# Reordering the attention turns of a two-layer macaron block: k, output projection, v's halves and a split evacuation

## The chip, the cores and the metric

One NeuronCore of a Trainium2 chip runs the whole program. The metric is device microseconds of one execution; the kernel before took 996.61 us (median of 3 runs, 995.93 to 996.84). The profile is of one further execution, of 997.68 us.

## The reference, cut to what matters

Activations are 4 sequences of 512 tokens of width 128. Layer 0 is half an FFN, attention, half an FFN; layer 1 is half a mixture of experts, attention, half a mixture of experts. Both attentions are causal with 16 heads of 64:

```python
q, k, v = x @ Wq, x @ Wk, x @ Wv                    # 128 -> 16 heads x 64
sim = where(causal, -max, q @ k.T * 64 ** -0.5)     # per head, 512 x 512
out = softmax(sim) @ v                              # row maxima are subtracted
out = sigmoid(x @ Wg) * out                         # in layer 0's attention alone
x = x + out @ Wout (+ b_out)                        # b_out in layer 1's attention
```

Every f32 matrix product is made of three f16 products: each operand is split into a high and a low half (high by high, high by low, low by high).

## The kernel before

An attention is 32 items: 4 sequences by 8 pairs of heads. An item passes six stages, one turn apart (`LAGS`): p projects q, k and v; m finds row maxima; s computes scores and exponentials; v multiplies by v's halves and evacuates; o splits the output in halves and turns it by a DMA; z is the output projection. `TURNS` is 37, and in turn t the item of stage p is t, of stage m is t-1, and so on. Turns 5 to 31 hold all six stages. All engines walk the same turns, each with its own instruction order written out by hand in a `body(t)`; semaphores tie them together. `FILL` puts a piece of other work (a transposition of normalized tokens, an FFN "up" or "down" projection, gate, routing) into some turns; `STATS` puts layer norm statistics at the end of some.

What the orders of one turn hold, with the lines of the profile:

- TensorE: scores(0) (L1926 to L1936), maxima(0) (L1890), project_q (L1735 to L1737, through `split_mm`), project_k, project_out (L1975 to L1977), scores(1), maxima(1), project_v, the fill, scores(2), maxima(2), outputs(0) (L1959 to L1961), max_rows (L1901), outputs(1). Where `late_k(a, t)` holds (stages p and s are present and the turn has no fill: 27 of 64 turns) project_k stands behind maxima(1) instead.
- ScalarE: exps(0) (L1009), q_high (L1030), k_high (L1035, behind exps(1) where late), output_high (L1042), exps(1), p_high (L1017), the fill's part, exps(2), minus_max (L1058), v_high (L1049), layer norm (L907), expert weight quarters (L954, L955, first attention, turns 2 to 25).
- VectorE: maxima(0) (L1345), q_low (L1352), k_low (L1358, behind maxima(2) where late), maxima(1), output_low (L1369), add_out (L1409, every eighth turn), maxima(2), the fill's part, evacuate (L1391 in the first attention alone, L1395, L1399), v_low (L1375), statistics (L1211, L1214).
- GpSimd: per item three subtractions for the low halves of the exponentials (L821) and two casts for high halves (L819); the quarters' low halves (L720) and the norm's rstd.
- SP: one transposing DMA per item (L626); it waits for output_low and for the project_out of the item before.

PSUM: q and v share bank 0, so project_q waits for v_low of the item before and project_v for q_low. k is in bank 7, which outputs(1) and the fill use too. So project_k waits for the last evacuation, and outputs(1) for k_low, or in turns with a fill for the fill's reader on VectorE. outputs(0) writes bank 6, outputs(1) bank 7; one evacuation, behind outputs(1), reads both. The output projection accumulates over eight items in bank 1. The scores use banks 4 and 5, so scores(u) waits for the exps before it. scores(0) waits for minus_max of its item, made in the turn before.

Of the kernel before, what the change touches and what calls it, by code (L numbers as in the profile page):

```python
# [24 lines left out]
ALU = mybir.AluOpType  # L25
# [6 lines left out]
def macaron_block(nc: bass.Bass, ins, out, phases):  # L32
    tokens = ins["L0_attn_tokens"]
    NB, SEQ, D = tokens.shape
    P = 128
    TOK = NB * SEQ
    NT = TOK // P
    TPB = SEQ // P
# [29 lines left out]
    with ctx:  # L68
# [3 lines left out]
        def sem(name):  # L72
            return ctx.enter_context(nc.semaphore(name))
# [263 lines left out]
        s_pl_last = sem("pl_last")  # L337
        s_pl = sem("pl")
        s_av_ps = sem("av_ps")

        s_o_f = sem("o_f")
        s_o_ev = sem("o_ev")
# [105 lines left out]
        def fill(a, t):  # L448
            return FILL[a].get(t, (None, None, None))
# [39 lines left out]
        def quarters(t):  # L489

            return (t - 2,) if 2 <= t < 26 else ()

        def late_k(a, t):

            p, m, s, v, o, z = items(t)
            return p is not None and s is not None and not fill(a, t)[0]

        def hidden(f, c, k):

# [11 lines left out]
        def items(t):  # L511

            return tuple(t - lag if 0 <= t - lag < ITEMS else None for lag in LAGS)
# [383 lines left out]
        def _(act):  # L897
# [99 lines left out]
            def attention(a, turns=range(TURNS)):  # L997
# [3 lines left out]
                def body(t):  # L1001
# [30 lines left out]
                    def k_high():  # L1032
                        j = base + p
                        act.wait_ge(s_k_ps, j + 1)
                        a_.activation(QKh[:, p % RING, 1], ps[:, k_bank(a, p), :], ACT.Copy, scale=1.0 / W_UP).then_inc(s_k_hi, 1)  # L1035
# [29 lines left out]
                        p_high()  # L1065
                    if p is not None:
                        q_high()
                        if not late_k(a, t):
                            k_high()
                    if o is not None:  # L1070
                        output_high()
                    if s is not None:
                        exps(1)
                        if late_k(a, t):
                            k_high()
                        if last:
                            p_high_last(1)
                        else:
                            p_high()
                    if kind == "turn":  # L1080
                        turned_x(n, c)
                    if kind == "up":
# [6 lines left out]
                        p_high_last(2)  # L1089
                    if m is not None:  # L1090
                        minus_max()
                    if p is not None:
                        v_high()
                    if t - 1 in STATS[a]:
                        normed(*STATS[a][t - 1])
                    if a == 0 and t == 0:
# [99 lines left out]
        def _(dve):  # L1196
# [127 lines left out]

            def attention(a, turns=range(TURNS)):
                base = a * ITEMS
                fb = 2 * ITEMS * a
                dve.wait_ge(s_att_set, 1)

                def body(t):  # L1330
# [48 lines left out]
                                                ALU.mult, ALU.subtract  # L1379
                                                ).then_inc(s_v_lo, 1)  # L1380

                    def evacuate():
                        j = base + v
                        dve.wait_ge(s_av_ps, j + 1)
                        o4 = ps[:, 6:8, 0:TPB * (DH + 1)].rearrange("p x (a b) -> p x a b", a=TPB)
                        den = o4[:, :, :, DH]
                        if a == 0:
                            q = seq_of(v) * TPB
                            h = (v % PAIRS) * 2
                            dve.wait_ge(s_g_one, seq_of(v) + 1)  # L1390
                            v_.tensor_tensor(osc[:, 0], den, gates[:, q:q + TPB, h:h + 2].rearrange("p a x -> p x a"),  # L1391
                                             ALU.mult).then_inc(s_o_f, 1)
                            dve.wait_ge(s_o_f, 2 * v + 1)
                            den = osc[:, 0]
                        v_.reciprocal(osc[:, 1], den).then_inc(s_o_f, 1)  # L1395
                        dve.wait_ge(s_o_f, fb + v + 1 if a else 2 * v + 2)
                        if v >= 1:
                            dve.wait_ge(s_o_lo, j)
                        v_.tensor_tensor(O32.rearrange("p a x c -> p x a c"), o4[:, :, :, 0:DH],  # L1399
                                         osc[:, 1].unsqueeze(3).broadcast_to([P, 2, TPB, DH]), ALU.mult  # L1400
                                         ).then_inc(s_o_ev, 1)

                    def add_out():
                        q = seq_of(z)
# [9 lines left out]
                        maxima(0)  # L1414
                    if p is not None:
                        q_low()
                        if not late_k(a, t):
                            k_low()
                    if m is not None:
                        maxima(1)  # L1420
                    if t == ITEMS + 3:
# [17 lines left out]
                        tiles_half(a, 0)  # L1439
                    if m is not None:  # L1440
                        maxima(2)
                    if late_k(a, t):
                        k_low()
                    if kind == "turn":
                        turned_x(n, c)
                    if kind == "up":
# [7 lines left out]
                    if t == ITEMS:  # L1454
                        chosen_half(a, 0)
                        hot_half(a, 0)
                    if v is not None:
                        evacuate()
                    if s == ITEMS - 1:
                        p_low_last()  # L1460
                    if p is not None:
                        v_low()
                    if a == 0 and t == 0:
                        gate_low()
                    if t in STATS[a]:
# [258 lines left out]
        def _(pe):  # L1724
# [93 lines left out]
            def attention(a, turns=range(TURNS)):  # L1818
# [3 lines left out]
                def body(t):  # L1822
# [118 lines left out]
                    def outputs(x):  # L1941
                        j, r, b = base + v, v % RING, v & 1
                        bank = 6 + x
                        if x == 0:
                            pe.wait_ge(s_pl, 3 * j + 3 - a - (v == ITEMS - 1))
                            if v == ITEMS - 1:
                                pe.wait_ge(s_pl_last, a + 1)
                            if v >= 1:
                                pe.wait_ge(s_o_ev, j)
                        elif fill(a, t)[0]:  # L1950
                            pe.wait_ge(*fill_read(a, t))
                        elif p is not None:
                            pe.wait_ge(s_k_lo, base + p + 1)
                        for i in range(TPB):
                            c = i * (DH + 1)
                            for k in range(i + 1):
                                at = KEY_AT[k] + (i - k) * P
                                ph_, pl_ = PH[:, b, x, at:at + P], PL[:, b, x, at:at + P]
                                mm(ps[:, bank, c:c + DH + 1], ph_, VH[:, r, k, x, 0:DH + 1], start=(k == 0), stop=False)  # L1959
                                mm(ps[:, bank, c:c + DH], ph_, VL[:, r, k, x, :], start=False, stop=False)  # L1960
                                ins_ = mm(ps[:, bank, c:c + DH + 1], pl_, VH[:, r, k, x, 0:DH + 1], start=False,  # L1961
                                          stop=(k == i))
                        if x == 1:
                            ins_.then_inc(s_av_ps, 1)

                    def project_out():
                        hp = z % PAIRS
# [15 lines left out]
                        maxima(0)  # L1983
                    if p is not None:
                        project_q()
                        if not late_k(a, t):
                            project_k()
                    if z is not None:
                        project_out()
                    if s is not None:  # L1990
                        scores(1)
                    if m is not None:
                        maxima(1)
                    if late_k(a, t):
                        project_k()
                    if p is not None:
                        project_v()
                    filled()
# [200 lines left out]
```

## Time and profile before

| | us |
|---|---|
| median of 3 runs | 996.61 |
| profiled execution | 997.68 |
| its span | 995.8 |
| first attention, scores of turn 2 to turn 32 | 49.8 to 343.9 |
| second attention, the same | 535.9 to 818.6 |

The span runs from the first to the last instruction. Matmuls are pipelined: one starts before the one in front ends, so the time from start to start tells what a group costs, and the idle time that the view shows in front of a matmul is somewhat less than what its start was late. Between the attentions lie mixture of experts stages, which the change doesn't touch.

### The profile page before, as it was taken

To read this page: it belongs to the slowest core of one execution; us is meant where nothing else is said; L and a number is where in the kernel's file an instruction comes from. 1 tells how busy PE (TensorE), PEld (TensorE's weight loads), DVE (VectorE), ACT (ScalarE), POOL (GpSimd) and SP (SyncE) were. 2 spreads that over 40 slices of the span, in tenths; PEclk is the share of its full clock that TensorE was granted. 3 is DMA by queue.
4 is the path that set the end of the run, shared out by engine and by line. 5 is a ranking of instruction groups with operands and counts; after the bars stand their busy time and mean duration, and the time that the engine had idled before them with its cause. 6 is when DMAs were issued, how large, how long until landed. Compare 5 with 4: busy or idle time off the path is not lost.

```text
span 995.8 us, 33341 instructions
## 1 busy us (share of the span) xinstructions
PE 867.2 (87%) x12904; PEld 613.3 (62%) x12904; DVE 763.7 (77%) x2338; ACT 688.7 (69%) x1183; POOL 738.2 (74%) x685
## 2 busy tenths in 40 slices
PE   5789998999898867999997898989989996799994
PEld 3556666666666654776763566666666664476663
DVE  6878888778778876897766778887887888695773
ACT  5688888878877634766775777777777774466662
POOL 6779989889878755676655988877877875577772
PEclk9999999999999987999998999999999999799997
DMA  4212322242225121223111111221221221212332
GB/s 154 53 41 70 35 66 48 52 76 34 34 24 129 23 34 31 65 52 91 47 33 51 24 23 35 23 45 35 23 45 35 24 44 34 54 50 50 94 71 83
DMA packets 88701, 50.55 MB, mean 51 GB/s; under 512 B 72162, under 2 KB 78050, under 8 KB 88548
## 3 DMA queue, kind: packets, MB, share of 16 engines
q1 hardware_dynamic: 81312, 35.29, 17.2%
q0 software_dynamic: 5888, 12.07, 4.9%
q8 instruction: 108, 1.77, 0.8%
q10 hardware_dynamic: 1348, 1.05, 0.3%
q14 instruction: 45, 0.37, 0.1%
HBM read 22.44 MB, written 9.18 MB: 32 GB/s over the span
## 4 chain that ended last, share of the span: by engine, by line
PE 53%; DVE 33%; issue 6%; ACT 3%; DMA 2%; POOL 1%; SPq 0%; POOLq 0%; DVEq 0%; ACTq 0%
DVE arena L1345 10%; PE ps L1735 8%; PE ps L1737 6%; PE ps L1736 6%; PE ps L1926 6%; PE ps L2158 4%; DVE arena L1375 4%; DVE arena L1369 3%; PE ps L1959 3%; DVE arena L1358 2%; PE ps L2171 2%; PE ps L1961 2%; PE ps L1890 2%; PE ps L2170 2%; PE ps L1960 2%
## 5 line engine op out<-in xcount | busy, mean ns | idle before, releaser
L821 POOL TENSOR_TENSOR arena<-arena 128x1024 f16<-128x1024 f32 x190 | 348.0, 1832 | 105.3 <-ACT arena L1017 94.6
L1345 DVE CUSTOM_DVE_ANT_0 arena<-ps,mask_qk 128x512 bf16<-128x512 f32 (+3 forms) x512 | 224.5, 485 | 37.8 <-PE ps L1890 36.7
L1009 ACT ACTIVATE arena<-ps,lift 128x1024 f32<-128x1024 f32 (+1 forms) x192 | 186.2, 970 | 81.4 <-PE ps L1936 79.4
L1926 PE MATMUL ps<-arena 64*128 64x512 f16 (+3 forms) x1536 | 150.7, 302 | 5.8 <-ACT arena L1009 3.0
L1959 PE MATMUL ps<-arena 128*128 128x65 f16 x1280 | 132.2, 196 | 21.6 <-DVE arena L1234 8.7
L1959 PEld LDWEIGHTS ps<-arena 128*128 128x128 f16 x1280 | 116.6, 98 | 38.6 <-DVE arena L1234 10.5
L872 POOL DMA_INDIRECT arena<-x_rows,arena x92 | 90.9, 988 | 62.0 <-PE ps L2133 25.4
L1960 PE MATMUL ps<-arena 128*128 128x64 f16 x1280 | 131.2, 194 | 0.0
L1961 PE MATMUL ps<-arena 128*128 128x65 f16 x1280 | 130.7, 194 | 0.0
L880 POOL DMA_INDIRECT y_rows<-arena x92 | 91.0, 989 | 43.5 <-issue 22.4
L1960 PEld LDWEIGHTS ps<-arena 128*128 128x128 f16 x1280 | 118.3, 99 | 0.2 <-issue 0.2
L1961 PEld LDWEIGHTS ps<-arena 128*128 128x128 f16 x1280 | 118.4, 98 | 0.0
L819 POOL CAST arena<-arena 128x1024 f16<-128x1024 f32 x124 | 102.4, 826 | 0.0
L1699 DVE SCALAR_TENSOR_TENSOR arena<-ps,arena 128x512 f32<-128x512 f32 x92 | 68.8, 748 | 24.9 <-ACT arena L1161 24.7
L1167 ACT ACTIVATE arena<-ps 128x512 f16<-128x512 f32 x92 | 54.9, 597 | 41.0 <-PE ps L2158 41.0
L1161 ACT ACTIVATE arena<-ps,arena 128x512 f32<-128x512 f32 x92 | 63.2, 687 | 25.7 <-PE ps L1737 25.5
L1705 DVE TENSOR_TENSOR arena<-ps,arena 128x512 f16<-128x512 f32 x92 | 63.3, 688 | 20.9 <-ACT arena L1167 20.4
L1926 PEld LDWEIGHTS ps<-arena 64*128 64x128 f16 x1536 | 52.5, 94 | 42.7 <-ACT arena L1009 13.9
L1058 ACT ACTIVATE arena<-ps 128x512 f16<-128x512 f32 x64 | 38.2, 597 | 47.2 <-PE ps L1901 47.1
L1890 PE MATMUL ps<-arena 64*128 64x512 f16 (+3 forms) x512 | 66.7, 298 | 3.6 <-DVE arena L1345 3.5
L2170 PE MATMUL ps<-E2h,arena 128*128 x368 | 67.4, 220 | 1.8 <-ACT arena L1175 1.1
L2171 PE MATMUL ps<-E2l,arena 128*128 x368 | 67.5, 219 | 0.0
(286 smaller groups left out, 2633.1 us busy)
## 6 DMA issues: line engine op xcount, KB each, us to landing
stage<-in_L_ffn_W SPq DMA_DIRECT2D x4, 1024.0 KB, 5.8
arena<-y_rows SPq DMA_DIRECT2D x14, 256.0 KB, 3.9
x_rows<-XN SPq DMA_DIRECT2D x8, 256.0 KB, 3.1
arena<-x_rows,arena POOLq DMA_INDIRECT x92, 2.8
y_rows<-arena POOLq DMA_INDIRECT x92, 2.5
stage<-in_L_attn_Wkv SPq DMA_DIRECT2D x2, 512.0 KB, 7.1
T<-arena SPq DMA_TRANSPOSE x64, 2.8
X<-in_L_attn_tokens SPq DMA_DIRECT2D x3, 256.0 KB, 5.5
```

The costliest lines, as they stand in the source:

```text
L819: g.tensor_copy(PH[:, b, :, cols], P32[:, :, cols]).then_inc(s_ph_pool, 1)
L821: g.tensor_tensor(PL[:, b, :, cols], P32[:, :, cols], PH[:, b, :, cols], ALU.subtract).then_inc(s_pl, 1)
L872: g.indirect_dma_start(XG[:, t % XRING, :], None, x_rows[t // HT], bass.IndirectOffsetOnAxis(ap=row_i[:, 0, t:t + 1], axis=0)).then_inc(s_ ...
L880: g.indirect_dma_start(y_rows, bass.IndirectOffsetOnAxis(ap=row_i[:, 1, t:t + 1], axis=0), YS[:, t % YRING, :], None).then_inc(s_y_out[t % ...
L1009: a_.activation(P32[:, :, UNIT_AT[u]:UNIT_AT[u] + UNIT_W[u]], ps[:, 4:6, 0:UNIT_W[u]], ACT.Exp, bias=lift[:]).then_inc(s_ex_p, 1)
L1345: v_.tensor_tensor_reduce(masked[:, x, 0:w], ps[:, 2 + x, at:at + w], mask_qk[:, CH - w:CH], 1.0, NEG, ALU.add, ALU.max, accum_out=MX[:, i ...
L1926: mm(ps[:, 4 + x, at:at + w], keys, queries, start=(n_ == 0 and part == 0), stop=False)
L1959: mm(ps[:, bank, c:c + DH + 1], ph_, VH[:, r, k, x, 0:DH + 1], start=(k == 0), stop=False)
L1960: mm(ps[:, bank, c:c + DH], ph_, VL[:, r, k, x, :], start=False, stop=False)
L1961: ins_ = mm(ps[:, bank, c:c + DH + 1], pl_, VH[:, r, k, x, 0:DH + 1], start=False, stop=(k == i))
L2170: mm(dst, GH[:, g, f, :], wh, start=(f == 0), stop=False)
L2171: mm(dst, GH[:, g, f, :], wl, start=False, stop=False)
```

## The change

On all three engines k follows q in every turn, so `late_k` goes. On TensorE the output projection moves from behind k to behind maxima(1). On ScalarE v_high moves ahead of the fill, exps(2) and minus_max; on VectorE v_low moves ahead of the evacuation. outputs(0) gets a semaphore of its own, and the evacuation runs once per head: head 0 when outputs(0) is done, head 1 when outputs(1) is. Each handles 4 denominators and 4 x 64 columns instead of 8 and 8 x 64.

```diff
+        s_av0_ps = sem("av0_ps")
...
@@ ScalarE
                     if p is not None:
                         q_high()
-                        if not late_k(a, t):
-                            k_high()
+                        k_high()
                     if o is not None:
                         output_high()
                     if s is not None:
                         exps(1)
-                        if late_k(a, t):
-                            k_high()
                         if last:
                             p_high_last(1)
                         else:
                             p_high()
+                    if p is not None:
+                        v_high()
...
                     if m is not None:
                         minus_max()
-                    if p is not None:
-                        v_high()
@@ VectorE
-                    def evacuate():
+                    def evacuate(x):
                         j = base + v
-                        dve.wait_ge(s_av_ps, j + 1)
-                        o4 = ps[:, 6:8, 0:TPB * (DH + 1)].rearrange("p x (a b) -> p x a b", a=TPB)
-                        den = o4[:, :, :, DH]
+                        n_ = fb + (4 if a == 0 else 2) * v + (2 if a == 0 else 1) * x
+                        dve.wait_ge(s_av_ps if x == 1 else s_av0_ps, j + 1)
+                        o3 = ps[:, 6 + x, 0:TPB * (DH + 1)].rearrange("p (a b) -> p a b", a=TPB)
+                        den = o3[:, :, DH]
                         if a == 0:
...
+                            v_.tensor_tensor(osc[:, 0, x], den, gates[:, q:q + TPB, h], ALU.mult).then_inc(s_o_f, 1)
...
+                        v_.reciprocal(osc[:, 1, x], den).then_inc(s_o_f, 1)
+                        dve.wait_ge(s_o_f, n_ + 1)
                         if v >= 1:
                             dve.wait_ge(s_o_lo, j)
...
+                        ins_ = v_.tensor_tensor(O32[:, :, x], o3[:, :, 0:DH],
+                                                osc[:, 1, x].unsqueeze(2).broadcast_to([P, TPB, DH]), ALU.mult)
+                        if x == 1:
+                            ins_.then_inc(s_o_ev, 1)
...
                     if p is not None:
                         q_low()
-                        if not late_k(a, t):
-                            k_low()
+                        k_low()
...
                     if m is not None:
                         maxima(2)
-                    if late_k(a, t):
-                        k_low()
...
+                    if p is not None:
+                        v_low()
                     if v is not None:
-                        evacuate()
+                        evacuate(0)
+                        evacuate(1)
                     if s == ITEMS - 1:
                         p_low_last()
-                    if p is not None:
-                        v_low()
@@ TensorE
-                        if x == 1:
-                            ins_.then_inc(s_av_ps, 1)
+                        ins_.then_inc(s_av_ps if x == 1 else s_av0_ps, 1)
...
                     if p is not None:
                         project_q()
-                        if not late_k(a, t):
-                            project_k()
-                    if z is not None:
-                        project_out()
+                        project_k()
                     if s is not None:
                         scores(1)
                     if m is not None:
                         maxima(1)
-                    if late_k(a, t):
-                        project_k()
+                    if z is not None:
+                        project_out()
                     if p is not None:
                         project_v()
```

## Rows read from the trace of the kernel before

Idle time in square brackets is that of the engine before the instruction, and what ended it.

**Rows 1.** The page: busy time of the engines; the DMA that transposes the outputs

```profile
PE 867.2 (87%) x12904; PEld 613.3 (62%) x12904; DVE 763.7 (77%) x2338; ACT 688.7 (69%) x1183; POOL 738.2 (74%) x685
...
T<-arena SPq DMA_TRANSPOSE x64, 2.8
```

**Rows 2.** The waits: who waited for whom: us, times, longest

```profile
POOL arena L821 <- ACT arena L1017: 94.6, 51, 9.8
...
PE ps L1735 <- DVE arena L1375: 33.2, 56, 1.7
```

**Rows 3.** Timeline of TensorE: start, us; an up turn, then a plain turn

```profile
183.61 0.38 PE L1735 MATMUL ps<-XTh,WQh 128*128 128x512 f16 x1 [0.69 <-DVE arena L1375]
...
678.30 0.82 PE L1926 MATMUL ps<-arena 64*128 64x512 f16 x6
...
679.21 0.38 PE L1890 MATMUL ps<-arena 64*128 64x512 f16 x2
680.00 0.39 PE L1735 MATMUL ps<-XTh,WQh 128*128 128x512 f16 x1 [0.41 <-DVE arena L1375]
...
680.66 0.22 PE L1975 MATMUL ps<-WOh,T 128*128 128x128 f16 x1
...
681.42 0.66 PE L1926 MATMUL ps<-arena 64*128 64x384 f16 x6
...
682.37 0.38 PE L1890 MATMUL ps<-arena 64*128 64x384 f16 x4
682.68 0.39 PE L1735 MATMUL ps<-XTh,WKh 128*128 128x512 f16 x1
...
684.11 0.50 PE L1926 MATMUL ps<-arena 64*128 64x256 f16 x6
...
685.74 0.40 PE L1901 MATMUL ps<-identh,arena 128*128 128x128 f16 x4
686.34 0.20 PE L1959 MATMUL ps<-arena 128*128 128x65 f16 x1 [0.20 <-DVE arena L1358]
...
687.35 0.82 PE L1926 MATMUL ps<-arena 64*128 64x512 f16 x6
```

**Rows 4.** Timeline of ScalarE: after stats, then the plain turn

```profile
161.73 1.64 ACT L907 ACTIVATE XN<-X,shift,rstd 128x128 f32<-128x128 f32 x4
...
679.41 1.11 ACT L1009 ACTIVATE arena<-ps,lift 128x1024 f32<-128x1024 f32 x1 [1.19 <-PE ps L1936]
...
686.17 0.60 ACT L1058 ACTIVATE arena<-ps 128x512 f16<-128x512 f32 x1 [0.48 <-PE ps L1901]
```

**Rows 5.** Timeline of VectorE in the plain turn

```profile
678.41 0.21 DVE L1395 RECIPROCAL arena<-ps 128x8 f32<-128x8 f32 x1 [1.18 <-PE ps L1961]
...
681.49 0.69 DVE L1352 SCALAR_TENSOR_TENSOR arena<-ps,arena 128x512 f16<-128x512 f32 x1 [0.33 <-ACT arena L1030]
682.79 0.56 DVE L1345 CUSTOM_DVE_ANT_0 arena<-ps,mask_qk 128x384 bf16<-128x384 f32 x1 [0.61 <-PE ps L1890]
...
685.60 0.69 DVE L1358 SCALAR_TENSOR_TENSOR arena<-ps,arena 128x512 f16<-128x512 f32 x1
```

**Rows 6.** Groups of VectorE by shape: count, busy, mean ns, idle before

```profile
L1399 DVE TENSOR_TENSOR arena<-ps,arena 128x512 f32<-128x512 f32 x64 | 44.2, 691 | 2.2
...
L1689 DVE TENSOR_TENSOR arena<-ps,arena 128x128 f16<-128x128 f32 x92 | 25.9, 282 | 10.1 <-ACT arena L1153 9.7
...
L1395 DVE RECIPROCAL arena<-arena 128x8 f32<-128x8 f32 x32 | 6.5, 203 | 1.1
...
L1391 DVE TENSOR_TENSOR arena<-ps,gates 128x8 f32<-128x8 f32 x32 | 5.3, 166 | 32.5 <-PE ps L1961 32.3
```

**Rows 7.** Timeline of TensorE: q behind a routing turn

```profile
670.96 0.38 PE L1735 MATMUL ps<-XTh,WQh 128*128 128x512 f16 x1 [1.57 <-DVE arena L1375]
```

**Rows 8.** Engines in turns 3 to 14 (window); GpSimd in an up turn (timeline)

```profile
58.20:172.90 114.70, 104.56 (x1902) 73.69 (x1900) 94.10 (x315) 96.97 (x155) 105.33 (x89) 0.99 0.23 46
...
188.95 2.15 POOL L821 TENSOR_TENSOR arena<-arena 128x1024 f16<-128x1024 f32 x1 [1.60 <-ACT arena L1017]
```

More of the change, by code:

```diff
@@ L491, in quarters @@
             return (t - 2,) if 2 <= t < 26 else ()
-        def late_k(a, t):
-            p, m, s, v, o, z = items(t)
-            return p is not None and s is not None and not fill(a, t)[0]
         def hidden(f, c, k):
@@ L1326, in attention @@
                 base = a * ITEMS
-                fb = 2 * ITEMS * a
+                fb = 4 * ITEMS * a
                 dve.wait_ge(s_att_set, 1)
@@ L1387, in evacuate @@
                         if a == 0:
                             q = seq_of(v) * TPB
-                            h = (v % PAIRS) * 2
+                            h = (v % PAIRS) * 2 + x
                             dve.wait_ge(s_g_one, seq_of(v) + 1)
-                            v_.tensor_tensor(osc[:, 0], den, gates[:, q:q + TPB, h:h + 2].rearrange("p a x -> p x a"),
-                                             ALU.mult).then_inc(s_o_f, 1)
-                            dve.wait_ge(s_o_f, 2 * v + 1)
@@ L1394, in evacuate @@
-                            den = osc[:, 0]
-                        v_.reciprocal(osc[:, 1], den).then_inc(s_o_f, 1)
-                        dve.wait_ge(s_o_f, fb + v + 1 if a else 2 * v + 2)
+                            v_.tensor_tensor(osc[:, 0, x], den, gates[:, q:q + TPB, h], ALU.mult).then_inc(s_o_f, 1)
+                            n_ += 1
+                            dve.wait_ge(s_o_f, n_)
+                            den = osc[:, 0, x]
+                        v_.reciprocal(osc[:, 1, x], den).then_inc(s_o_f, 1)
@@ L1397, in evacuate @@
+                        dve.wait_ge(s_o_f, n_ + 1)
                         if v >= 1:
                             dve.wait_ge(s_o_lo, j)
-                        v_.tensor_tensor(O32.rearrange("p a x c -> p x a c"), o4[:, :, :, 0:DH],
-                                         osc[:, 1].unsqueeze(3).broadcast_to([P, 2, TPB, DH]), ALU.mult
-                                         ).then_inc(s_o_ev, 1)
+                        ins_ = v_.tensor_tensor(O32[:, :, x], o3[:, :, 0:DH],
+                                                osc[:, 1, x].unsqueeze(2).broadcast_to([P, TPB, DH]), ALU.mult)
```

## The prediction, made before the kernel ran

> **What bounds the kernel now.** I read the page, then the waits, then single turns of the timeline. The page's totals [rows 1] give TensorE 867.2 of 995.8 us and VectorE, GpSimd and ScalarE 764, 738 and 689: no engine is full, so what counts is who waits for whom. The waits [rows 2] show the pattern that the change aims at: TensorE's q projection waited 56 times, 33.2 us, for line 1375 (v's low half), which stands behind the evacuation on VectorE. GpSimd's largest wait, 94.6 us, is for ScalarE's line 1017: it has room on the whole, though not everywhere.
>
> One turn of the second attention (678.30 to 687.35, 9.05 us) [rows 3] shows the size. TensorE starts first scores at 678.30, first maxima at 679.21, q at 680.00. The second maxima, also 512 columns, let their follower start after 0.31 (682.37 to 682.68), so q could have started at 679.52: 0.48 lost, of which the view prints 0.41 as idle. Max rows start at 685.74; its four 128-column matmuls need some 0.25 (twelve such of the output projection take 0.76), the second head's outputs start at 686.34: 0.35 lost, waiting for k's low half, line 1358. Without both the turn is 9.05 - 0.83 = 8.22 us. TensorE's own work, with these two waits in it, bounds a turn.
>
> **Part by part, for such a plain turn.** Times from here on are us from the turn's first scores.
>
> *v's halves ahead of the evacuation.* The q wait goes if v's low half is done before TensorE's next q. TensorE in the new order: maxima at 0.91, q 1.22, k 1.88 (pitch 0.66, as q to output projection in rows 3), scores(1) 2.54, maxima(1) 3.49, output projection 3.80, v 4.56 (0.76), scores(2) 5.33 (v and k together 1.43 from 682.68 to 684.11), max rows 6.96 (1.63 as 684.11 to 685.74), second outputs 7.21, next turn 8.22.
>
> *k behind q in every turn* (27 of 64 turns had it late: 6 in the first attention, 21 in the second). It frees the outputs' wait of 0.35 but puts k's low half ahead of the second maxima on VectorE. exps(0) starts at 1.11 and takes 1.11 [rows 4]; q's high half follows from about 2.1 to 2.7 (0.60, like the copy at 686.17), q's low half 2.76, k's low half 3.37 to 4.06 (0.69 each, pitch 0.61), second maxima from 3.98, where TensorE has them ready at 3.91. From there to the end of the third maxima VectorE took 2.81 (682.79 to 685.60) [rows 5], so 6.79, the accumulator read 6.87, max rows 6.93: against TensorE's 6.96. It fits with 0.03 to spare; bounds: no delay, and 0.6 (a whole low half) if nothing of it is covered. I take 0.03 late on average. Minus-max on ScalarE then ends at about 8.0, 0.2 ahead of the next scores. k's wait for bank 7 asks for the previous turn's evacuation, done at about 0.8, k starts at 1.88: free.
>
> *Output projection behind the second maxima.* The same twelve matmuls, 0.76, moved past scores(1) and maxima(1), so these start earlier. Queues: SP's transposing DMA waits for this projection before it refills OT; the projection ends near 4.7, output_low at about 6, so SP does not wait longer; the DMA lands 2.8 us later [rows 1], some 3 us ahead of the next projection. In the last turns of each attention, where TensorE waits for that DMA, the move hides a little. Zero in full turns, 0 to 1 us each in two tails.
>
> *Evacuation head by head.* The old one took 0.21 + 0.69 and a pause of some 0.04 between them (an estimate from the timeline of rows 5). Half the product: 282 ns for 128 columns and 691 for 512 of the same kind [rows 6], so 0.42 for 256, twice 0.84, +0.15. The reciprocal of 4 columns is not shown; bounds 0 and 0.20 as for 8 columns; I take 0.20 (a size of 8 is all fixed cost). With 0.04 between dependents VectorE gets +0.4 us per item in the second attention and, with one more small product (0.17), +0.6 in the first: 32 us in all. Where is it hidden? Head 0 runs beside head 1's matmuls; behind those, VectorE has 0.21 + 0.04 + 0.42 = 0.67, before 0.94 + 0.61 for v's low half. In a plain turn VectorE waits 0.33 us for q's high half, 0.61 for the second maxima and 1.18 for the outputs [rows 5]: it has the room. If that cover is gone (routing, stats) the extra is paid in full.
>
> A rule speaks against this part. The Trainium skill, VectorE: DVE Perf Modes, section Rules for kernel authors, says to minimize the count of operations, since each drains the pipe; by it, 160 more instructions at the 0.17 to 0.2 us of rows 6 would add about 30 us. Its page Perfetto Trace Analysis, section Optimizing Scalar/DVE Operations, says the other way: where such an engine isn't full but causes bubbles, breaking instructions up can finish work sooner. The waits of rows 2 and 5 bear out the second for plain turns.
>
> **Sum over the turns** (turns 3 to 31 of each attention, full or nearly).
> Second attention: 7 plain turns (11, 17 to 19, 25 to 27) x 0.8 = 5.6. 9 turns with stats or an add to X on VectorE x 0.6 = 5.4 (0.6 more work sits in the chain to max rows, part of what is won is lost). 6 turns with a transposition: only the q wait, 0.48, less a little: 2.8; their outputs(1) waits for the transposition's low half, which stays behind the third maxima. 3 pairs of a routing turn and the next: before, q started 1.57 late [rows 7]; now v's low half stands ahead of the evacuation, so q comes some 0.9 earlier, but VectorE, with the evacuation's extra, holds the rest: 1.3, 1.3 and 0.6 = 3.2. First turns 0.9. Together 17.9.
> First attention, turns 3 to 14: GpSimd is busy 105.3 of 114.7 us here [rows 8]; it splits the expert weights beside its usual work. Of 9.4 idle, some 3 are 0.08 us pauses between dependents, so at most 6.4 can go, whatever TensorE wins (12 x 0.7 = 8.4). After stats, ScalarE also has the normalization, 1.64 [rows 4], and two weight copies ahead of exps(0). I take 4.5 (bounds 0 and 6.4).
> Turns 15 to 31: 8 turns with an up projection, q gap 0.69 [rows 3], really 0.76: 8 x 0.75 = 6.0. 9 others x 0.6 = 5.4. Tails 1.
> Sum 17.9 + 4.5 + 11.4 + 1 = 34.8. Several covers are 0.03 to 0.2 us wide, about the reading error, so I take a tenth off: 31.3. The profiled execution took 997.7 us (span 995.8): 966.4. The median before, 996.6, is 1.1 lower: 965.3, rounded to 965.5.
>
> **Rivals.**
> (a) GpSimd takes over for good in the first attention: turns 3 to 26 stay at its pace and win only 3 us rather than 12 (4.5, 6.0 and a part of the others). For: rows 8. Against: in an up turn it still waited 1.60 us for line 1017 [rows 8]. 31.3 - 9 gives 974. Chance 0.14.
> (b) VectorE becomes the bound in all turns but the plain ones, since k's low half and the extra evacuation meet: turns gain half. 981. For: the 0.03 margin. Against: the waits in rows 5. Chance 0.11.
> (c) Slower: the chain exps(0), q and k halves, second and third maxima, max rows closes over TensorE. It decides when exps(0) starts later than 1.1 by more than the 0.03 margin in most turns: then the 27 formerly late k turns pay 0.61 each (16.5), and the 64 split evacuations their 0.4 or 0.6 (32), against 33.2 [rows 2] and 27 x 0.20 [rows 3] of idle removed: +10, 1007. For: VectorE is busy 77% already [rows 1]. Against: in rows 4 exps(0) starts straight behind the scores, and VectorE idles [rows 5]. Chance 0.05. It is where the Trainium skill's rule of few operations (VectorE: DVE Perf Modes) would point.
> (d) The q wait doesn't go: it passes to v's high half on ScalarE, itself behind p's high half. Then only the outputs' 0.35 in 27 turns is won: 9.5 us, 987. Against: v's high half would end near 6.3, q is at 9.4. Chance 0.04.
> The forecast has 0.66.
>
> **How the numbers follow.** A measurement here tells about 0.2% (2 us) from no change. Forecast, (a), (b) and (d) are faster, though I leave 0.03 for a change that other stages swallow: faster 0.91, same 0.03, slower 0.06. Range: with every term at its upper bound (0.83 in all but the transposition turns, GpSimd's 6.4, 2 for the tails, nothing taken off) 43 us go, 953.5; that they all come together is unlikely, so the low end is 956.5. High end takes in (b): 982. About 1 in 10 is left out above and a little below.
>
> **What would show it.** Right: q on TensorE starts about 0.3 after the first maxima with no release by v's low half; second outputs follow max rows without a gap in turns without a fill; plain turns of 8.2 to 8.3 us; the wait of line 1735 for v's low half gone from the waits; VectorE's busy time up by about 30 us. Wrong: max rows waiting for the third maxima in plain turns (b, c), k waiting for the evacuation, outputs of head 0 waiting for GpSimd's low halves outside the first attention (a), or plain turns above 8.6 us.

## The result and the profile after

| kernel | median of 4 runs, us | ratio to before, 95% interval | profiled span |
|---|---|---|---|
| before, beside it | 996.27 (995.35 to 996.84) | | 995.8 |
| changed | 961.55 (960.31 to 962.96) | 0.9653 [0.9636, 0.9669] | 959.6 |

The change takes 34.7 us off the median; 965.5 us had been predicted, a gain of 31.3.

The page of the changed kernel, busy time of the engines and the largest group of GpSimd:

```profile
PE 855.4 (89%) x12904; PEld 606.6 (63%) x12904; DVE 784.8 (82%) x2498; ACT 683.2 (71%) x1183; POOL 743.8 (78%) x685
...
L817 POOL TENSOR_TENSOR arena<-arena 128x1024 f16<-128x1024 f32 x190 | 351.8, 1852 | 64.0 <-ACT arena L1013 53.3
```

VectorE has 160 instructions more and is busy 21 us longer than in [rows 1]; TensorE's busy time fell by 12. The q projection (now line 1728) waited 56 times, 33.2 us, for v's low half (now line 1368) in [rows 2]; in the changed kernel it waits 4 times, 1.9 us in all. In the waits (who waited for whom: us, times, longest) the first line is GpSimd's largest (94.6 us before); the two largest that are left to TensorE in the attention turns are for the exponentials and for the maxima:

```profile
POOL arena L817 <- ACT arena L1013: 53.3, 38, 9.4
...
PEld ps L1919 <- ACT arena L1005: 38.4, 69, 1.3
...
PE ps L1919 <- ACT arena L1005: 11.5, 19, 1.2
...
PE ps L1894 <- DVE arena L1338: 11.5, 17, 1.9
```

The plain turn of [rows 3], in the changed kernel's timeline of TensorE (start, us):

```profile
654.13 0.82 PE L1919 MATMUL ps<-arena 64*128 64x512 f16 x6
...
655.04 0.38 PE L1883 MATMUL ps<-arena 64*128 64x512 f16 x2
655.35 0.39 PE L1728 MATMUL ps<-XTh,WQh 128*128 128x512 f16 x1
...
656.00 0.38 PE L1728 MATMUL ps<-XTh,WKh 128*128 128x512 f16 x1
...
656.75 0.66 PE L1919 MATMUL ps<-arena 64*128 64x384 f16 x6
...
657.70 0.38 PE L1883 MATMUL ps<-arena 64*128 64x384 f16 x4
658.01 0.23 PE L1967 MATMUL ps<-WOh,T 128*128 128x128 f16 x1
...
659.46 0.50 PE L1919 MATMUL ps<-arena 64*128 64x256 f16 x6
...
661.09 0.40 PE L1894 MATMUL ps<-identh,arena 128*128 128x128 f16 x4
661.32 0.19 PE L1952 MATMUL ps<-arena 128*128 128x65 f16 x1
...
662.32 0.39 PE L1919 MATMUL ps<-arena 64*128 64x512 f16 x2
```

No row has idle time in brackets. q starts 0.31 behind the first maxima, k 0.65 behind q, the output projection behind the second maxima, the second head's outputs 0.23 behind max rows. The turn lasts 8.19 us; 8.22 was predicted.

VectorE in the same turn (timeline), as in [rows 5]:

```profile
654.24 0.18 DVE L1389 RECIPROCAL arena<-ps 128x4 f32<-128x4 f32 x1 [0.25 <-PE ps L1954]
654.45 0.42 DVE L1393 TENSOR_TENSOR arena<-ps,arena 128x256 f32<-128x256 f32 x1
655.46 0.69 DVE L1338 CUSTOM_DVE_ANT_0 arena<-ps,mask_qk 128x512 bf16<-128x512 f32 x1 [0.58 <-PE ps L1883]
...
656.86 0.69 DVE L1345 SCALAR_TENSOR_TENSOR arena<-ps,arena 128x512 f16<-128x512 f32 x1
657.48 0.69 DVE L1351 SCALAR_TENSOR_TENSOR arena<-ps,arena 128x512 f16<-128x512 f32 x1
658.12 0.56 DVE L1338 CUSTOM_DVE_ANT_0 arena<-ps,mask_qk 128x384 bf16<-128x384 f32 x1
```

It idles 0.83 us where it idled 2.1: q_low, k_low and the second maxima follow without a pause, and TensorE waits for none of them. The half evacuation costs 0.18 + 0.42.

Below, a turn's length goes from the start of its first exponentials, exps(0), to that of the next turn's. "Turns" are the sums over turns 2 to 32 of the first and second attention: 303.3 and 294.0 before, 289.9 and 272.6 after. The profiled spans differ by 36.2 us: start 0.9, first attention 13.4, between 1.6, second attention 21.3, end -1.0.

### The profile page after: what moved, and what is told of

Same layout as the page of the kernel before. It is cut to its first block and busy times, and to the rows that moved or that the text cites. A ratio compares the mean times of both kernels' runs of the same rounds, so it can differ in the third digit from the quotient of the medians.

```text
span 959.6 us, 33597 instructions
## 1 busy us (share of the span) xinstructions
PE 855.4 (89%) x12904; PEld 606.6 (63%) x12904; DVE 784.8 (82%) x2498; ACT 683.2 (71%) x1183; POOL 743.8 (78%) x685
## 5 line engine op out<-in xcount | busy, mean ns | idle before, releaser
L817 POOL TENSOR_TENSOR arena<-arena 128x1024 f16<-128x1024 f32 x190 | 351.8, 1852 | 64.0 <-ACT arena L1013 53.3
L1919 PE MATMUL ps<-arena 64*128 64x512 f16 (+3 forms) x1536 | 148.1, 298 | 14.4 <-ACT arena L1005 11.5
L1953 PEld LDWEIGHTS ps<-arena 128*128 128x128 f16 x1280 | 118.8, 99 | 0.1
L1883 PE MATMUL ps<-arena 64*128 64x512 f16 (+3 forms) x512 | 66.1, 295 | 3.8 <-DVE arena L1338 3.6
```

Of the source, the lines that this page charges most:

```text
L817: g.tensor_tensor(PL[:, b, :, cols], P32[:, :, cols], PH[:, b, :, cols], ALU.subtract).then_inc(s_pl, 1)
L1919: mm(ps[:, 4 + x, at:at + w], keys, queries, start=(n_ == 0 and part == 0), stop=False)
```

## The experiments

Ratios are to the kernel before on the same chip. The edits are to the changed kernel, but for one (e5). Most are shown as a summary of calls in their order, with dots for what is left out; the two with code are cut. The last column is the length of a plain turn of the second attention, one with no fill, stats or add, as in [rows 3]. Each run has one trace, and turns are read from it.

| run | median, us | ratio, 95% interval | turns, us | plain turn |
|---|---|---|---|---|
| changed, again | 995.39 | 0.9661 [0.9636, 0.9685] | 290.0, 272.7 | 8.19 |
| e2 whole evacuation | 1001.31 | 0.9716 [0.9693, 0.974] | 294.2, 270.5 | 8.19 |
| e6 quarters moved | 995.53 | 0.9662 [0.9636, 0.9688] | 287.1, 272.6 | 8.19 |
| e7 e6 + e2 | 1000.48 | 0.9704 [0.9678, 0.973] | 294.3, 270.5 | 8.19 |
| e1 k late | 971.60 | 0.9766 [0.9748, 0.9784] | 290.2, 282.5 | 8.87 |
| e3 v behind | 981.60 | 0.9865 [0.9848, 0.9882] | 305.9, 278.9 | 8.38 |
| e4 output projection in front | 980.23 | 0.9851 [0.9831, 0.9872] | 295.5, 286.2 | 8.72 |
| e5 v ahead alone (on before) | 974.93 | 0.9803 [0.9783, 0.9823] | 293.1, 278.7 | 8.57 |
| e9 e2 + GpSimd waits | 965.01 | 0.9692 [0.9678, 0.9706] | 290.5, 271.6 | 8.20 |
| e10 GpSimd waits | 962.74 | 0.9670 [0.9654, 0.9686] | 289.9, 271.6 | 8.19 |
| e11 e6 + GpSimd waits | 958.42 | 0.9626 [0.9611, 0.9642] | 286.8, 271.5 | 8.19 |
| e12 e11 + e2 | 961.55 | 0.9660 [0.9646, 0.9674] | 287.3, 271.6 | 8.19 |

The first four ran on a chip where the kernel before took 1032.07 us. In the traces of the changed kernel on the two chips, the stages outside the attention turns are 37 us longer on this one. Its attention turns are the same to 0.02 us, but for two of the second attention that offset each other: turn 2 took 8.26 us here and 9.14 there, turn 32 took 11.30 and 10.45.

### One part undone, or alone

**e1, k late again.**

```diff
+ def late_k(a, t):  # turn with a projection and scores, TensorE not filled otherwise
-   project_q(); project_k();             ...; maxima(1); project_out()
+   project_q(); if not late: project_k(); ...; maxima(1); if late: project_k()
+   project_out()          # k_high behind exps(1), k_low behind maxima(2) when late
```

> The changed kernel with k late again in the 27 turns without a fill (behind the second maxima on TensorE, behind exps(1) on ScalarE, behind the third maxima on VectorE). Theory: with the q wait gone, scores(1) would then stand right behind q, at about 1.9 us of the turn, and wait for exps(0), which ends at 2.2: 0.3 to 0.4 in 21 and 6 turns, 8 to 10 us more than the changed kernel, ratio to before 0.973 to 0.976; plain turns of the second attention 8.5 to 8.6 us. Rival (my prediction's reason, outputs(1) waits 0.35 for k's low half): the same size, but the idle time stands before outputs(1) instead of scores(1). Second rival (k's place does not matter once q is free): plain turns 8.2.

0.9766, 11 us slower than the changed kernel by the ratios (0.0113 of 996): just above the 0.973 to 0.976 expected, which the interval reaches (from 0.9748). But a plain turn is 8.87, 0.68 longer where 0.3 to 0.4 was expected, with both theories' waits in it; the first attention's turns lose only 0.3 us in all. Timeline of TensorE:

```profile
658.66 0.66 PE L1930 MATMUL ps<-arena 64*128 64x384 f16 x6 [0.23 <-ACT arena L1010]
...
664.25 0.20 PE L1963 MATMUL ps<-arena 128*128 128x65 f16 x1 [0.20 <-DVE arena L1359]
```

The outputs wait for k's low half, as before, and scores(1), which now follow q at once, come too early for the exponentials that free their bank. With k ahead of them, k fills that time.

**e3, v's halves behind the evacuation.**

```diff
-   v_low(); evacuate(0); evacuate(1); p_low_last()
+   evacuate(0); evacuate(1); p_low_last(); v_low()      # and v_high behind minus_max
```

> The changed kernel with v's low half behind the (split) evacuation on VectorE and v's high half behind minus-max on ScalarE, as before. Theory: q waits again for v's low half, but less than before since only head 1's piece stands ahead of it: 0.2 us per full turn in the second attention, 0.4 in the first, 15 to 20 us more than the changed kernel, ratio 0.980 to 0.986; plain turns 8.4. Rival (q's wait alone is what the change removed, the split does nothing for it): 33 us more, ratio near 1.0, plain turns 8.7.

0.9865, just above the 0.980 to 0.986 expected, plain turns 8.38 as expected. The wait is back, in the waits:

```profile
PEld ps L1728 <- DVE arena L1368: 31.9, 53, 2.9
...
PE ps L1728 <- DVE arena L1368: 17.5, 31, 2.6
```

It is short in plain turns (0.11 us idle) and long where VectorE has stats or routing. Three turns of the first attention (20, 21, 28) are 13.39, 11.23 and 12.13 us, against 10.32, 9.44 and 9.27. In turns 20 and 28, 6 us together, this trace has the effect of the section after next (output_low takes 2.53 and 2.54 us there), so not all of the 21 us is the order of v itself. In turn 21 output_low takes its usual 0.69; what made that turn longer was not traced.

**e4, output projection in front of scores(1).**

```diff
-   project_q(); project_k(); scores(1); maxima(1); project_out()
+   project_q(); project_k(); project_out(); scores(1); maxima(1)
```

> The changed kernel with the output projection ahead of scores(1) again. Theory: the second maxima reach VectorE 0.76 later, at 4.7 us of a plain turn, past the 4.0 at which VectorE is free, so max rows wait 0.65 in turns without a fill, 0.1 to 0.2 with a transposition or a route, nothing with an up projection: plain turns 8.85, 15 to 18 us more in all, ratio 0.980 to 0.984. Rival (the move only hides the DMA in the tails): plain turns 8.2, 1 us more, ratio 0.966.

0.9851, just above the 0.980 to 0.984 expected (the interval starts at 0.9831), a plain turn 8.72 rather than 8.85. The wait that I had expected, 0.65 at max rows, is not what the timeline of TensorE has. Its one idle time in a plain turn stands ahead of scores(2), which need exps(1), late because scores(1) are:

```profile
669.66 0.50 PE L1919 MATMUL ps<-arena 64*128 64x256 f16 x6 [0.21 <-ACT arena L1005]
```

They start 5.60 us into the turn (5.33 in the changed kernel), max rows 7.47 instead of 6.96. So half of the 0.5 us arises between the two, where the view shows no idle time; that half is not explained.

**e5, v ahead alone**, on the kernel before.

```diff
-   ...; minus_max(); v_high()           # ScalarE
+   v_high(); ...; minus_max()
-   evacuate(); p_low_last(); v_low()    # VectorE
+   v_low(); evacuate(); p_low_last()
```

> The kernel before with one part of the change alone: v's high half ahead of the fill and exps(2), v's low half ahead of the whole evacuation. Theory: the q wait (33.2 us of idle) goes, the other waits stay: outputs(1) 0.35 in late k turns; 25 to 30 us less than before, ratio 0.970 to 0.975, plain turns 8.55. Rival (the parts work only together, k and scores then wait for each other): less than 15 us, ratio above 0.985.

0.9803: slower than the 0.970 to 0.975 expected and between the theories, 20 us of the 35. A plain turn wins 9.05 - 8.57 = 0.48, the very term of the prediction; the 0.20 idle ahead of the outputs stays (timeline of TensorE):

```profile
668.89 0.20 PE L1959 MATMUL ps<-arena 128*128 128x65 f16 x1 [0.20 <-DVE arena L1358]
```

The other parts then bring the plain turn to 8.19: 0.38 more, where 0.35 had been predicted. So the parts are not additive: undone one at a time the three moves (e1, e3, e4) cost 0.0113, 0.0212 and 0.0198 of the time before, 11, 21 and 20 us, 52 in all, where the whole change gives 35. The traces of e1, e3 and e4 each show a wait of TensorE that the changed kernel doesn't have. Some 6 of the 52 are the two turns of e3 named above, so the sum exceeds 35 without them too.

### The split evacuation and the quarters

**changed, again**, for the other chip.

> The changed kernel itself, as the yardstick for the three that run beside it: ratio to the kernel before 0.965, plain turns of the second attention 8.19 to 8.20 us.

The ratio repeats: 0.9661 after 0.9653.

**e2, evacuation whole again**, behind v's low half.

```diff
-   evacuate(0); evacuate(1)
+   evacuate()        # one reciprocal of 8, one product of 512 columns
```

> The changed kernel with one evacuation for both heads, as before (v's low half still ahead of it). Theory: in a plain turn the whole evacuation ends 1.05 us into the next turn and k starts at about 1.9, so plain turns stay at 8.19 to 8.20 us; VectorE loses about 21 us of busy time, all of it hidden; in turns after stats the piece behind the second outputs is 0.27 longer. Total within 2 us of the changed kernel, ratio to before 0.964 to 0.967. Rival (the split is what frees the turn): k or the first maxima wait for the evacuation in each of about 58 turns, 0.3 us each, ratio 0.98. Second rival (VectorE is a bound, the added small operations cost): 5 to 10 us faster than the changed kernel, ratio 0.955 to 0.960.

0.9716: the theory's 0.964 to 0.967 is missed, and so are both rivals. Plain turns are the same to 0.01, so the split neither costs nor gives there. The median is 5.9 us worse. Against the changed kernel on this chip, turns 20 and 28 of the first attention are 2.0 and 3.1 us longer: 12.32 and 12.40 against 10.32 and 9.28. Turn 32 of the second is 3.0 shorter, 8.29 against 11.30 (10.45 on the other chip). My theory named none of these; see the next section. Turns 9, 13, 21 and 29 of the second, each behind stats, are 0.28 longer, the piece of 0.27 that the expectation names; 16 and 24, behind routing, are 0.26 shorter. All turns together are only 2.1 us longer; where the other 3.8 of the median arise is not shown.

**e6, expert quarters out of the turns behind stats.** GpSimd idled 9.4 of 114.7 us in turns 3 to 14 [rows 8]; in the changed kernel 3.6 of 111.0 (window: us, busy by engine, GpSimd last):

```profile
56.60:167.60 111.00, 102.77 (x1902) 72.55 (x1900) 100.11 (x351) 96.34 (x154) 107.37 (x90) 1.00 0.23 48
```

```diff
-   return (t - 2,) if 2 <= t < 26 else ()
+   free = [u for u in range(2, ITEMS) if u not in (4, 7, 9, 13, 20, 21)]
+   return (free.index(t),) if t in free else ()
-   expert_block at t in (6, 10, 14, 18); second layer at 27
+   expert_block at t in (8, 14, 19, 25); second layer at 33
```

> The changed kernel with the expert weights' quarters left out of turns 4, 7, 9, 13, 20 and 21 of the first attention (those in which ScalarE normalizes), and taken up to turn 31 instead of 25; the loads of the blocks and the second layer's load move along. Theory: in turns 5, 8, 10, 14, 21 and 22 TensorE's second scores waited 0.36 to 0.85 us for exps(0), which stood behind the normalization and two copies; without the copies exps(0) starts 1.0 earlier, these waits go: 4 to 5 us less in the first attention, ratio 0.960 to 0.962. Rival (GpSimd is the bound of turns 3 to 14): the waits move to outputs(0) or exps(0) for GpSimd's low halves; since fewer quarters fall in these turns it would win even more, 6 to 8 us. Second rival (neither: TensorE and VectorE bound these turns): within 1 us of the changed kernel.

Turns 2 to 14 went from 118.8 to 115.7, short of the 4 to 5 us expected; turns 20 and 21 won 1.6 more, turns 28 and 29 gave 1.4 back. All turns together are 3.0 us shorter, yet the total, 0.9662, can't be told from the changed kernel's 0.9661: the 0.960 to 0.962 expected didn't come, and by the total alone the second rival stands. In a turn behind stats, ScalarE has the normalization and two quarter copies ahead of exps(0), and scores(1) wait for it. The timeline of TensorE in turn 5, changed kernel:

```profile
76.21 0.66 PE L1919 MATMUL ps<-arena 64*128 64x384 f16 x6 [0.85 <-ACT arena L1005]
```

and with the quarters moved:

```profile
75.91 0.66 PE L1920 MATMUL ps<-arena 64*128 64x384 f16 x6 [0.44 <-ACT arena L1006]
```

Over turns 3 to 14, TensorE's idle time put down to the exponentials falls from 3.5 to 0.9 us. In neither kernel is any put down to GpSimd directly. As the edit relieves both engines, it doesn't prove that ScalarE alone was the limit.

**e7, both.**

> Both edits at once: quarters moved and the whole evacuation. Theory: the sum of the two, 4 to 6 us below the changed kernel, ratio 0.959 to 0.962. If the split evacuation matters only where VectorE is full, it shows as a difference to the run with moved quarters alone of 0 to 2 us.

0.9704, where 0.959 to 0.962 was expected: turns 20 and 28 are 12.19 and 12.32. Moving the quarters does not mend what the whole evacuation does to them.

### Which of two instructions starts first

In turn 20 the difference is one instruction. These are VectorE's low half of the outputs (both inputs in SBUF) and GpSimd's subtraction, in the timeline of the changed kernel:

```profile
219.71 0.68 DVE L1362 TENSOR_TENSOR arena<-arena 128x512 f16<-128x512 f32 x1
...
219.72 2.66 POOL L817 TENSOR_TENSOR arena<-arena 128x1024 f16<-128x1024 f32 x1
```

with the whole evacuation (e2), VectorE, GpSimd, and TensorE's max rows:

```profile
220.08 2.46 DVE L1361 TENSOR_TENSOR arena<-arena 128x512 f16<-128x512 f32 x1
...
219.86 2.13 POOL L816 TENSOR_TENSOR arena<-arena 128x1024 f16<-128x1024 f32 x1
...
223.88 0.40 PE L1890 MATMUL ps<-identh,arena 128*128 128x128 f16 x4 [2.36 <-DVE arena L1337]
```

Whoever starts first runs at its own length. The other lasts until the first is done and then its own length, nearly: 219.86 + 2.13 = 221.99, and VectorE ends at 222.54, 0.55 later. In the changed kernel VectorE was first, by 0.01 us; in e2 GpSimd, by 0.22. VectorE's loss is TensorE's: the third maxima stand behind it on VectorE, and max rows wait for them. In turn 28 e2 has the same (2.46). So the split matters there by who is early. In turn 32 of the second attention the changed kernel loses (VectorE, GpSimd):

```profile
786.70 2.60 DVE L1362 TENSOR_TENSOR arena<-arena 128x512 f16<-128x512 f32 x1
...
786.62 2.13 POOL L817 TENSOR_TENSOR arena<-arena 128x1024 f16<-128x1024 f32 x1 [0.99 <-ACT arena L1013]
```

while with the whole evacuation VectorE starts its low half 0.18 us ahead of GpSimd, and it takes 0.69. The kernel before lost this race too, in its own turn 32:

```profile
823.28 2.48 DVE L1369 TENSOR_TENSOR arena<-arena 128x512 f16<-128x512 f32 x1
```

The Trainium skill, SBUF — State Buffer, section Who interferes with whom, states that a VectorE instruction with two SBUF inputs contends with a GpSimd instruction that reads SBUF, for a port pair that they share and that is an exclusive lock, and that issue order decides who blocks. The trace agrees, with the durations above: in the changed kernel all 12 low halves of the outputs that took over 1.2 us started while a GpSimd `tensor_tensor` with two SBUF inputs ran, and the 32 that started while GpSimd ran nothing took 0.68 to 0.69.

The test: let GpSimd's first subtraction of an item, the long one, wait for VectorE's low half of that turn. Undisturbed, the low half takes 0.69 us, and GpSimd had been waiting for ScalarE in many turns anyway (line 1013, 38 times in the waits above).

```diff
+   if u == 0 and o is not None:
+       pool.wait_ge(s_o_lo, ITEMS * a + o + 1)
    g.tensor_tensor(PL[:, b, :, cols] ...
```

**e9**, with the whole evacuation:

> The kernel of e2 (changed kernel, whole evacuation) in which GpSimd's first subtraction of an item also waits for the output's low half (output_low) of that turn on VectorE. Theory: where GpSimd's 2.13 us subtraction starts a little ahead of output_low, output_low takes until it ends (2.46 instead of 0.69 us in turns 20 and 28 of the first attention, 1.89 in turn 29), and max rows wait for it; with the order fixed output_low takes 0.69 there, turn 20 goes from 12.3 to 10.5, turn 28 from 12.4 to 10, and the whole evacuation is then as good as the split one or better: 4 to 6 us less than e2 in the attentions, ratio 0.960 to 0.966. Rival (the split evacuation itself gave the 2 and 3 us in turns 20 and 28, through the 0.27 us shorter piece ahead of the statistics): these turns stay at 12.3 and 12.4, ratio 0.968 or more, since GpSimd now waits too.

Turns 20 and 28 fall from 12.32 and 12.40 to 10.55 and 9.51, as the theory has it and the rival doesn't; turn 29 falls from 11.30 to 10.40. But turns 11, 12 and 14 are 0.5 us longer each, all turns together are 2.7 shorter where 4 to 6 was expected, and the total, 0.9692, misses the 0.960 to 0.966. Timeline of turn 20, VectorE and GpSimd:

```profile
221.34 0.69 DVE L1363 TENSOR_TENSOR arena<-arena 128x512 f16<-128x512 f32 x1
...
222.18 2.14 POOL L818 TENSOR_TENSOR arena<-arena 128x1024 f16<-128x1024 f32 x1 [0.82 <-DVE arena L1363]
```

**e10**, with the split evacuation:

> The changed kernel with the same wait. Theory: it had lost this race in turn 29 of the first attention (1.90) and in turns 32 and 33 of the second (2.60, 2.13), so these lose 1.2, 1.9 and 0.3 us; in plain turns GpSimd starts 0.25 later, inside its idle 0.9: 3 us less than the changed kernel, ratio 0.962 to 0.964. Rival (GpSimd's start is what counts): plain turns above 8.2, slower than the changed kernel.

Turn 29 of the first attention 11.75 to 10.83, turn 32 of the second 10.45 to 8.83; but turns 7, 11 and 12 lose 0.3 to 0.5 each and 16 and 24 of the second 0.28. The sums are 289.9 and 271.6; the total, 0.9670, shows no gain. The expected 3 us didn't come. Over the 64 items the low half took 57.1 us in the changed kernel and 54.2 here, against 44 (64 x 0.69) undisturbed. The wait guards one of GpSimd's instructions, and others still hold it: the expert quarters' low halves (line 716) and the 512-column subtraction of the item before. In turn 11 a quarter's low half starts 0.04 us ahead, and VectorE's takes 1.66 us where it took 0.85. The other longer turns were not traced; that GpSimd starts later in them is a guess.

**e11**, e10 and the quarters moved:

> The changed kernel with the quarters moved (as e6) and the same wait: the sum of both, 3 us less for the quarters and 3 to 5 for the wait (output_low took 2.53 in turn 29 of e6): 6 to 8 us less in the attentions than the changed kernel, ratio 0.957 to 0.960. If the wait holds GpSimd back in the first attention, less than 3.

958.42, 0.9626 [0.9611, 0.9642]: the fastest of all, 4.3 us below e10 on the same chip, short of the 0.957 to 0.960 expected. The gain is in turns 2 to 14 (119.2 to 116.3). The interval overlaps a little with the changed kernel's, which ran at another time, so that the two edits beat the changed kernel is likely but not shown.

**e12**, e11 with the whole evacuation:

> Quarters moved, whole evacuation and the wait together. Theory: the split by itself is worth nothing once the race is fixed, so this is within 2 us of the kernel before it in this list (quarters moved and the wait); where VectorE is full (behind the routing turns) it is up to 1 us faster. Rival (the split matters by itself): 4 us or more behind.

961.55, 3.1 us behind e11, between theory and rival. The turns are only 0.5 us longer than e11's; in the two traces 2.3 us lie between the attentions, and why is not settled. So with GpSimd's wait in place, splitting the evacuation is worth 0.5 to 0.6 us in the turns (561.4 against 562.0 between e10 and e9), and 2 to 3 in the medians (962.74 against 965.01, where the intervals overlap, and 958.42 against 961.55, where they don't).

## Why the prediction was right

**q wait, 0.48; outputs' wait, 0.35.** Shown: e5 wins 0.48, the rest 0.38, and the plain turn is 8.19 against 8.22. But the 0.35 needs more than k's new place: with the output projection left in front (e4) a plain turn is 8.72. The prediction's part on that move said zero in full turns, though its schedule of a turn relied on it: undoing it costs 20 us. The seven plain turns give 6.0 us (5.6 predicted).

**k_low ahead of the second maxima, covered by 0.03.** Held: in the plain turn shown above, k's low half starts 3.35 us into the turn, the second maxima 3.99 and max rows 6.96, where 3.37, 3.98 and 6.96 were predicted, and TensorE waits for none of them. I had let turns with stats or an add win only 0.6 of 0.83, as if k's low half were partly uncovered; seven of the nine won 0.88, two (4 and 7) nothing: 6.0 for 5.4.

**Transposition and routing turns.** 3.9 for 2.8, but unevenly: turn 5 alone won 2.0 and turn 8 0.1, the other four 0.46 each. 5.5 for 3.2 in the routing pairs: the q wait behind a routing turn, 1.57 in [rows 7], is 0.30 in the changed kernel (turn 16; the same in 24), and k waits 0.20 for the evacuation behind it:

```profile
646.80 0.38 PE L1728 MATMUL ps<-XTh,WQh 128*128 128x512 f16 x1 [0.30 <-DVE arena L1368]
```

The first turns lost 0.2 rather than winning 0.9; most of that is turn 2, which the trace on the other chip has 0.9 shorter. The second attention's turns, 21.3 for 17.9, are the largest miss of the sum, to the good side.

**First attention.** Turns 3 to 14 gave 3.7 for 4.5. Turns 15 to 31: up projections 5.5 for 6.0, the nine others 3.0 for 5.4. The tail turns 2 and 32 gave 1.3 for 1. Most of the missing 2.4 is turn 29, 1.89 longer than before. There k waits 0.66 for the evacuation, and the low half lasts 1.90 behind GpSimd (timeline, VectorE then GpSimd):

```profile
306.24 1.90 DVE L1362 TENSOR_TENSOR arena<-arena 128x512 f16<-128x512 f32 x1
...
305.45 2.13 POOL L817 TENSOR_TENSOR arena<-arena 128x1024 f16<-128x1024 f32 x1 [0.44 <-ACT arena L1013]
```

With GpSimd behind it (e10) the turn is 10.83, still 0.97 over before. That VectorE and GpSimd block each other stood nowhere in the prediction. It is a step that was missing: at turn 29 it costs some 0.9 us of the gain, and at turn 32 of the second attention 1.6 us (e10) stay unwon, as the kernel before was held there too. At turns 20 and 28 it cost nothing, by luck: in turn 20 VectorE was first by 0.01 us. Waits of k for the evacuation, which the prediction had called free, are there as well, but in few turns.

**VectorE's busy time** rose 21 us, not 30. By groups, the split adds 24.1: products 10.1, reciprocals 9.6 (0.18 each and not 0.20, half a product 0.42 as said), the small product of the first attention 4.4. Low halves held by GpSimd add 7.0 (57.1 against 50.1 us before). Other groups took 10 us less, which was not traced.

**The tenth taken off** (3.5) was not needed: the sum before it, 34.8, is what was measured. That agreement of totals is partly luck, as +3.4 in the second attention stands against -0.8 and -2.9 in the first. The trace's turns give 34.7 and its whole span 36.2.

**The rivals.** (b) and (c) fall with the unbroken rows of the plain turn and the gains of the others; (d) with the q wait, 33.2 us down to 1.9. The Trainium skill's rule of few operations (VectorE: DVE Perf Modes, section Rules for kernel authors) doesn't show in the time here: 160 more instructions left plain turns at 8.19 (e2 and the changed kernel alike), and behind stats the split won 0.28. (a) was half right: GpSimd is 97% busy in turns 3 to 14, and relieving it and ScalarE together (e6) gives 3 us. But the turns with an up projection behind turn 14 won their 0.67 each. GpSimd's late subtractions did hold the exponentials in seven places of the changed kernel, 4.5 us of ScalarE's idle time, nearly all in early turns of the second attention.

## What to carry to other kernels

Look for the work that stands between a producer and the wait for it in an engine's queue, and move the short one that others wait for ahead of the long one that nobody does: putting v's low half back behind the evacuation, or the output projection back in front of the scores, cost some 20 us here, though no engine was full. The parts of a reordering are neither additive nor safe alone, so price the finished order, turn by turn. Where VectorE has an instruction with two SBUF inputs on the critical path and GpSimd runs long ones, compare their starts in the trace: 0.2 us of shift elsewhere moved a turn by 2 us.

## What the hardware showed unexpectedly

The 0.69 us low half lasted up to 2.60 us when GpSimd's subtraction was first, and that subtraction 2.66 instead of 2.13 when it was second. Two kernels that differ only in the evacuation thus differed by 2.0 and 3.1 us in two turns, and by 3.0 the other way in a third.

Two chips ran the same kernel before at 996 and 1032 us; the ratio of the changed kernel was the same on both, 0.9653 and 0.9661. In the changed kernel's traces all but two attention turns are equal to 0.02 us, and the difference lies in the stages outside. Why these differ was not looked into.
